# A two-layer graph network on one core: who copies edge weights and who adds them up in the sparse attention stage

## What is computed

```python
q = (z @ Wq.T + bq).reshape(n, H, D)          # n = 1250, H = 8, D = 64
k = (z @ Wk.T + bk).reshape(n, H, D)
v = (z @ Wv.T + bv).reshape(n, H, D)
s = einsum('ehd,ehd->eh', q[src], k[dst]) / sqrt(D) + att_bias   # one row per edge
m = segment_max(s, src)
p = exp(s - m[src])
denom = segment_sum(p, src)
alpha = p / where(denom[src] == 0, 1.0, denom[src])
agg = segment_sum(alpha[:, :, None] * v[dst], src)
att = agg.reshape(n, C) @ Wo.T + bo
x = x + att
```

## Time and profile before

| | us |
|---|---|
| median of 3 runs (2309.41 to 2314.92) | 2309.54 |
| the profiled execution, as timed | 2305.52 |
| its span in the profile | 2303.5 |
| busy: PE / DVE / ACT / POOL | 2067.1 / 1332.7 / 725.7 / 765.4 |
| attention stage, first multiply to last multiply | 681 to 1030 |

### The profile page before, as it was taken

The page is one execution under the profiler, slowest core; times in us unless marked ns, Lnnn a source line. Parts: engine busy times, 40 slices in busy tenths (PEclk is TensorE's granted clock), DMA queues, the critical chain, the costliest instruction groups (busy, mean ns, idle before and its releaser), DMA issues.

```text
span 2303.5 us, 31178 instructions
## 1 busy us (share of the span) xinstructions
PE 2067.1 (90%) x11980; PEld 1262.7 (55%) x11980; DVE 1332.7 (58%) x3173; ACT 725.7 (32%) x1551; POOL 765.4 (33%) x524
## 2 busy tenths in 40 slices
PE   4998987898988579998999999999999999999977
PEld 3555554443335345555775456677777754455554
DVE  5665687878969557772224544442222234279997
ACT  4221122320015345431222355554211102135552
POOL 1346878887864576450000000000000000014443
PEclk9998998999989889999999999999999999999999
DMA  9994232223249769655000010002200005000000
GB/s 321 386 374 105 13 66 3 3 3 65 3 69 219 149 160 242 176 148 176 1 1 10 1 74 1 1 1 92 92 1 1 1 6 145 0 1 10 10 14 14
DMA packets 105266, 181.95 MB, mean 79 GB/s; under 512 B 64600, under 2 KB 66290, under 8 KB 94910
## 3 DMA queue, kind: packets, MB, share of 16 engines
q1 hardware_dynamic: 60047, 178.50, 24.8%
q0 software_dynamic: 45072, 1.46, 5.7%
HBM read 109.21 MB, written 70.71 MB: 78 GB/s over the span
## 4 chain that ended last, share of the span: by engine, by line
PE 64%; DVE 10%; POOL 8%; DMA 8%; ACT 5%; issue 4%; SPq 2%; DVEq 0%; PEldq 0%; ACTq 0%; POOLq 0%; PEld 0%
PE banks L203 19%; POOL edge_table L622 7%; PE banks L2395 6%; PE banks L2437 6%; DMA edge_table<-arena 6%; PE banks L2821 3%; PE banks L1746 3%; PE banks L2223 2%; PE banks L2211 2%; PE banks L2198 2%; PE banks L197 2%; PE banks L1545 2%; PE banks L2247 2%; PE banks L1566 2%; DVE arena L1445 1%
## 5 line engine op out<-in xcount | busy, mean ns | idle before, releaser
L622 POOL DMA_INDIRECT edge_table<-arena x313 | 523.5, 1673 | 268.8 <-DMA edge_table<-arena 155.7
L203 PE MATMUL banks<-arena 128*125 128x512 f32 x1200 | 555.3, 609 | 16.9 <-DVE arena L3041 15.1
L203 PEld LDWEIGHTS banks<-arena 128*125 128x125 f32 x1200 | 221.7, 193 | 262.8 <-issue 244.9
L1445 DVE TENSOR_TENSOR arena<-banks,arena 125x1000 f32<-125x1000 f32 x100 | 193.9, 1955 | 82.8 <-POOL arena L1481 36.6
L2848 POOL CAST arena<-arena 125x128 f32<-125x128 uint32 x10 | 2.9, 292 | 699.5 <-DVE arena L2984 699.5
L1545 PE MATMUL banks<-arena 64*125 64x250 f32 x800 | 115.4, 408 | 67.3 <-DVE arena L1445 62.8
L2343 DVE SCALAR_TENSOR_TENSOR arena<-banks,arena 125x512 f32<-125x512 f32 x80 | 60.1, 751 | 189.4 <-PE banks L2437 189.4
L1481 POOL TENSOR_TENSOR arena<-arena 125x1000 f32<-125x1000 f32 x56 | 132.5, 2438 | 84.5 <-DVE arena L1445 84.5
L2395 PEld LDWEIGHTS banks<-arena 128*128 128x128 f32 x1280 | 144.0, 192 | 6.7 <-issue 6.6
L2090 DVE CUSTOM_DVE_ANT_0 arena<-banks,arena 125x512 f32<-125x512 f32 (+8 forms) x144 | 73.0, 553 | 128.7 <-PE banks L2198 125.9
L2395 PE MATMUL banks<-arena 128*128 128x125 f32 x1280 | 146.4, 276 | 0.1
(11 more groups left out here) (372 smaller groups left out, 3376.5 us busy)
## 6 DMA issues: line engine op xcount, KB each, us to landing
edge_table<-arena SPq DMA_DIRECT2D x23, 2304.0 KB, 25.9
arena<-edge_table SPq DMA_DIRECT2D x50, 984.4 KB
arena<-L_ffn_W SPq DMA_DIRECT2D x4, 2048.0 KB, 10.0
arena<-edge_table SPq DMA_DIRECT2D x50, 114.3 KB
adjacency<-arena SPq DMA_DIRECT2D x50, 109.4 KB
arena<-adjacency SPq DMA_DIRECT2D x10, 546.9 KB
edge_table<-arena POOLq DMA_INDIRECT x313
arena<-x SPq DMA_DIRECT2D x1, 2240.0 KB
```

The costliest lines, as they stand in the source:

```text
L203: last = nc.tensor.matmul(dst, xT[:, i, :], w[:, i, 0:n], start=(i == 0), stop=(i == k - 1))
L622: pool.indirect_dma_start(d["table"], bass.IndirectOffsetOnAxis(ap=cell[0:EP, c:c + 1].bitcast(U32), axis=0), vals[0:EP, c * ROW:(c + 1) * ...
L1445: nc.vector.tensor_tensor(weights_of(m).rearrange("p (s e n) -> p s e n", s=2, e=2), unit_scores(m).rearrange("p e (s n) -> p s e n", s=2) ...
```

## The change

Five things are changed at once.

1. A new ACT instruction for every unit (`copy_weights`) copies the four heads' weights of the block out of their nine-word records into a contiguous buffer (`copy_g[m % 2]`, 125x1000 fp32, head by head). It stands ahead of the unit's exponential in ACT's order and waits for the block to have landed and for the multiply of unit `m - 2`. DVE's multiply reads this buffer in place of the block, and waits for it (`a_w`).
2. `att_pool` is gone. DVE does `sum_weights` in all ten passes.
3. A block is loaded in three parts of 84, 83 and 83 sources, six DMAs in place of two.
4. SP loads block `i + 3` as soon as both copies and the gather of block `i` are done, and only then waits for the counts and stores them. The gather of a block now stands behind the exponential of its first unit.
5. X is stored by tiles, ten `spread`s in place of one.

```diff
             sp.wait_ge(g_ev, 3 * TILES)
-            spread(sp, d["x_kept"], X[0:TP, :, :].rearrange("p t c -> p (t c)"), s_x)
+            for t in range(TILES):
+                spread(sp, d["x_kept"][:, t * C:(t + 1) * C], X[0:TP, t, :], s_x)
...
+        BLOCK_PARTS = ((0, 84), (84, 167), (167, CHUNK))
...
-                spread(sp, edge_block(i)[0:TP, :, :], table[tok(b), sources(c), :], s_tab[i % RING])
+                for v, w in BLOCK_PARTS:
+                    spread(sp, edge_block(i)[0:TP, v:w, :], table[tok(b), c * CHUNK + v:c * CHUNK + w, :], s_tab[i % RING])
...
             for i in range(BLOCKS):
                 c, b = chunk_and_tile(i)
+                if i + RING < BLOCKS:
+                    sp.wait_ge(a_w, 2 * (i + 1))
+                    sp.wait_ge(a_ca, i + 1)
+                    load_block(i + RING)
                 sp.wait_ge(a_cc, i + 1)
                 spread(sp, adj_v[c][:, :, tok(b)], count_g[i % 2][0:TP, :, :], s_adj[i % 2])
-                if i + RING < BLOCKS:
-                    sp.wait_ge(a_p, 2 * (i + 1))
-                    load_block(i + RING)
...
-                if h == 0:
-                    block_loaded(dve, m // 2)
...
+                dve.wait_ge(a_w, m + 1)
                 dve.wait_ge(a_e, m + 1)
                 nc.vector.tensor_tensor(
                     weights_of(m).rearrange("p (s e n) -> p s e n", s=2, e=2),
                     unit_scores(m).rearrange("p e (s n) -> p s e n", s=2),
-                    edge_block(m // 2)[0:TP, :, 4 * h:4 * h + 4].rearrange("p n (s e) -> p s e n", s=2),
+                    copy_g[m % 2][0:TP, :].rearrange("p (s e n) -> p s e n", s=2, e=2),
                     ALU.mult).then_inc(a_p, 1)
-                if m >= 1 and place(m - 1)[1] and place(m - 1)[0] < DVE_PASSES:
-                    sum_weights(nc.vector, dve, m - 1)
+                if m >= 1 and place(m - 1)[1]:
+                    sum_weights(dve, m - 1)
...
+            def copy_weights(m):
+                h = place(m)[2]
+                if h == 0:
+                    block_loaded(act, m // 2)
+                if m >= 2:
+                    act.wait_ge(a_p, m - 1)
+                nc.scalar.activation(copy_g[m % 2][0:TP, :].rearrange("p (j n) -> p n j", j=4),
+                                     edge_block(m // 2)[0:TP, :, 4 * h:4 * h + 4], ACT.Copy).then_inc(a_w, 1)
...
-                if i >= 1 and h == 0:
-                    gather(i)
-                if m == 1:
-                    gather(0)
+                copy_weights(m)
                 act.wait_ge(a_s, m + 1)
                 nc.scalar.activation(unit_scores(m), unit_scores(m), ACT.Exp).then_inc(a_e, 1)
-                if h == 0 and i >= 1:
-                    count_out(i - 1)
+                if h == 0:
+                    gather(i)
+                    if i >= 1:
+                        count_out(i - 1)
```

More of the change, by code:

```diff
@@ L124, in gps_two_layers @@
         s_const = sem("constants_ready")
-        s_x = sem("x_loaded")
+        s_x = sem("x_loaded_and_stored")
+        X_STORED = 32 + 32 * TILES
         z_rows, z_turned, z_cols = sem("z_ready"), sem("z_transposed"), sem("zT_ready")
@@ L1300, in gps_two_layers @@
         assert 33792 + 2 * CHUNK * ROW <= 36864 + CLEAR * ROW
-        DVE_PASSES = 3
         values_kept = arena[:, 0:CHUNKS * PAIRS * CHUNK].rearrange("p (c j n) -> p c j n", c=CHUNKS, j=PAIRS)
@@ L1305, in gps_two_layers @@
         count_g = [space.take(CHUNK).rearrange("p (u n) -> p u n", u=2) for _ in range(2)]
-        space = Space(BUF, BUF + 4616)
+        copy_g = [space.take(4 * CHUNK)]
+        space = Space(BUF, BUF + 4616 + 240)
         plain_g = [space.take(CHUNK) for _ in range(2)]
@@ L1309, in gps_two_layers @@
         rden = space.take(CHUNK)
+        copy_g.append(space.take(4 * CHUNK))
         s_tab = [sem(f"table_block_loaded_{i}") for i in range(RING)]
@@ L1315, in gps_two_layers @@
         a_e = sem("att_exponentials_ready")
+        a_w = sem("att_edge_weights_copied")
         a_p = sem("att_weights_ready")
@@ L1360, in sources @@
             return slice(c * CHUNK, (c + 1) * CHUNK)
+        BLOCK_PARTS = ((0, 84), (84, 167), (167, CHUNK))
         def block_loaded(eng, i):
-            eng.wait_ge(s_tab[i % RING], 32 * (i // RING + 1))
+            eng.wait_ge(s_tab[i % RING], 32 * len(BLOCK_PARTS) * (i // RING + 1))
         def att_sp(sp):
@@ L1396, in att_sp @@
                 if v == 1:
-                    sp.wait_ge(s_x, 96)
+                    sp.wait_ge(s_x, X_STORED + 32)
                 spread(sp, flat_x[:, a:b], d["x_kept"][:, a:b], s_x)
@@ L1462, in att_dve @@
                                 divide(g - CHUNKS - 1, half)
+            sum_weights(dve, UNITS - 1)
             for u in range(2):
@@ L1471, in att_dve, with sum_weights @@
             leave_stage(dve, "DVE")
-        def sum_weights(ops, eng, m):
+        def sum_weights(dve, m):
             g, n, h = place(m)
-            eng.wait_ge(a_p, m + 1)
+            dve.wait_ge(a_p, m + 1)
             if n == 1:
-                eng.wait_ge(a_pv, m - 1)
+                dve.wait_ge(a_pv, m - 1)
             else:
-                eng.wait_ge(a_sum, m - 2 * (g + 1) - 1)
+                dve.wait_ge(a_sum, m - 2 * (g + 1) - 1)
             total_p = psum_g[g % 2][0:TP, 2 * h:2 * h + 2, :].rearrange("p s n -> p (s n)")
-            ops.tensor_tensor(total_p, total_p, weights_of(m), ALU.add).then_inc(a_sum, 1)
-        def att_pool(pool):
-            pool.wait_ge(a_sum, ADDS * DVE_PASSES)
-            for m in range(PER * DVE_PASSES, UNITS):
-                if place(m)[1]:
-                    sum_weights(nc.gpsimd, pool, m)
+            nc.vector.tensor_tensor(total_p, total_p, weights_of(m), ALU.add).then_inc(a_sum, 1)
         def att_act(act):
@@ L1493, in copied @@
                 if g == 0:
-                    act.wait_ge(s_x, 64)
+                    act.wait_ge(s_x, X_STORED)
                 out = qT_g[:, :, sources(c)] if late else values_kept[:, c, :, :]
@@ L1498, in copied @@
                                      .rearrange("p b (j n) -> p b j n", j=2), ACT.Copy).then_inc(a_raw, 1)
+            def copy_weights(m):
[6 more added lines that the diff above has]
+                                     edge_block(m // 2)[0:TP, :, 4 * h:4 * h + 4], ACT.Copy).then_inc(a_w, 1)
             def gather(i):
                 c, b = chunk_and_tile(i)
-                block_loaded(act, i)
                 if i >= 2:
@@ L1679, in ff_dve @@
                 if t == 0:
-                    dve.wait_ge(s_x, 96)
+                    dve.wait_ge(s_x, X_STORED + 32)
                 if t == X_EARLY:
-                    dve.wait_ge(s_x, 128)
+                    dve.wait_ge(s_x, X_STORED + 64)
                 link(dve, nc.vector.tensor_tensor(X[0:TP, t, :], X[0:TP, t, :], XN[0:TP, t, :], ALU.add))
@@ L3275, in _ @@
             edges_pool(pool)
-            att_pool(pool)
             causal_pool(pool)
```

## The result

| | before | after |
|---|---|---|
| median, us (5 executions each, side by side) | 2309.41 | 2294.72 (2293.42 to 2296.95) |
| profiled execution, us | 2305.52 | 2294.18 |
| its span, us | 2303.5 | 2292.4 |
| busy PE / DVE / ACT / POOL, us | 2067.1 / 1332.7 / 725.7 / 765.4 | 2073.3 / 1316.2 / 898.0 / 629.5 |

The ratio of the times is 0.9935, with an interval of 0.9912 to 0.9957. The kernel became faster by 0.65%, some 15 us by the medians and 11.3 us between the two profiled executions. The forecast was 2269 us, a gain of 40. So the sign and the range held, and the size was off by 26 us. The 4 us by which I raised the sum to a median were therefore mostly chance, and the gain against those medians is nearer to 10 us.

The account below looks back on a forecast made before the run. Taken as bounds: a 36 us stall on POOL's order, DVE in early passes, PE in later ones. From 2305.5 us, -37 up to pass 6 and -3 late give 2265, plus 4.0 for the median 2269 us; range 2256 to 2313.

Parts of the forecast that it names:

- The 4 us by which I raised the sum to a median: Whole kernel: 2265 us summed from the profiled execution became 2269, since the earlier median stood 4.0 us above that execution.
- The copy: New ACT instruction per unit: 1.1 us each, between bounds of 1.03 and 2.0, making ACT's block about 5.5 us.
- The start: Unit 0: copy and exponential now stand behind block 0's landing, 1.1 + 1.0 and half a us for issues, +2.6 us.
- The sum: First multiply to pass 6: 2.6 + 16 x 5.9 + 14 x 5.5 = 174 us against 211.5, -37; late passes -3.
- The doubled copy: Rival, chance 0.22: scattered writes make ACT's copy 1.95 us; 2321 us, turning to loss at about 1.85 us a copy.
- The late passes: Passes 6 to 9: the shorter DVE multiply counts once a pass behind the inverse, -0.8 us each, -3 in all.
- The stall: Attention stage: 36.0 us of waiting for POOL's sum, queued behind its scatters, is freed with the sums on DVE.
- The term of 7 us: Store of X near 544: packets of 2048 bytes save POOL some 7 us of its 12, four scatters, leaving 39 at 681.
- The part on the blocks: Scatters beside block loads in 3024-byte parts: 5.1 us for two in flight, 2.5 us a scatter, against 3.8 before.
- my 778: Table scatters: the remaining 39 at 2.5 us each end at about 778, before block 25 is wanted (about 805).
- DMA as the limit: Rival, chance 0.15: added small packets at 0.1 us each make blocks 6.3 us, 7.5 beside scatters; 2293 us.
- The term of 5.9 us a block: First 16 attention blocks: loads slowed by scatters, 4.99/0.84 = 5.9 us a block, making DMA the limit above ACT's 5.5.

Follow-up runs that it names:

- large packets: The changed kernel with blocks loaded whole (9000 bytes) and X stored whole (20480 bytes): median 2296.2 us, ratio 0.9959.
- half early, all late: The changed kernel with copies for the second unit of each block only in passes 0 to 5, all in passes 6 to 9: 2263.2 us, ratio 0.9814.
- the same with whole blocks: The kernel "half early, all late" with blocks loaded whole, X still stored by tiles: 2286.6 us, ratio 0.9926.
- the kernel with pairs: The changed kernel with two heads' words side by side in the copy buffer, DVE reading with 8-byte stride: 2257.8 us, ratio 0.9794.

## Why the prediction was right in sign and wrong in size

*The copy: the step that failed.* The term was 1.1 us for a copy. The trace has 1.90 us for the first one, which stands alone (the timeline under "The start"), and 2.117 on average. Timeline of ACT over a block of pass 1, and a copy of pass 7:

```profile
734.75 2.09 ACT L1508 ACTIVATE arena<-arena 125x1000 f32<-125x1000 f32 x1
736.51 1.22 ACT L1531 ACTIVATE banks<-banks 125x1000 f32<-125x1000 f32 x1
737.53 2.08 ACT L1508 ACTIVATE arena<-arena 125x1000 f32<-125x1000 f32 x1
739.27 1.23 ACT L1531 ACTIVATE banks<-banks 125x1000 f32<-125x1000 f32 x1
740.29 0.78 ACT L1515 ACTIVATE arena<-arena 125x250 f32<-125x250 f32 x1
740.83 0.33 ACT L1515 ACTIVATION_READ_ACCUMULATOR arena<-arena 125x1 f32 x1
740.92 0.51 ACT L1522 ACTIVATE arena<-banks 125x250 f32<-125x250 f32 x1
741.18 2.10 ACT L1508 ACTIVATE arena<-arena 125x1000 f32<-125x1000 f32 x1
...
930.10 1.97 ACT L1508 ACTIVATE arena<-arena 125x1000 f32<-125x1000 f32 x1
```

I had both bounds, 1.03 and 2.0 us, and chose the lower end by DVE's fill of one word in nine. It was the wrong neighbour: another engine, and no input to read. The right one was ACT's own row with scattered writes, line 554, which I had priced at 1.8 ns an element; the copy has (1900 - 205)/1000, 1.7. A rule for the next time is to take the neighbour on the same engine and with the same side strided, even where its type differs. The Trainium skill ("SBUF — State Buffer", section "Door 1: The DMA port swizzle") asks for at least two hits on each line of 16 bytes. The runs agree, for ACT's writes as for DVE's reads: with one word in a line the copy takes 1.90 us alone and the multiply 1.967, and two words side by side are enough (1.185 and 1.193 us).

*The sum.* From 734.75 to 741.18 a block takes 6.43 us, and with a fifth of the values' copy (1.0 us) 6.63, that is 33.2 a pass. The sum had 5.9 for 16 blocks and 5.5 for 14, on average 5.71. Timeline of DVE at the first multiply of pass 6, before and after:

```profile
886.80 1.98 DVE L1445 TENSOR_TENSOR arena<-banks,arena 125x1000 f32<-125x1000 f32 x1 [0.67 <-ACT banks L1524]
...
879.55 1.20 DVE L1452 TENSOR_TENSOR arena<-banks,arena 125x1000 f32<-125x1000 f32 x1 [0.44 <-ACT banks L1531]
```

From the first multiply at 682.05 the thirty blocks took 197.5 us, where the sum had 171.4: 26.1 us more. A second step failed as well, in the base of the sum. I read the start of pass 6 as 892.5, the end of a stretch in the earlier trace rows, but its first multiply starts at 886.80. So before, the thirty blocks took 205.8 us and not 211.5, and the forecast held 5.7 us of gain that wasn't there. The start took 1.1 us and not 2.6, and from pass 6 to the end 3.9 us were gained and not 3. So of the sum's 40.5 us (37.5 and 3) there remain 40.5 - 26.1 - 5.7 + 1.5 + 0.9 = 11.1, and the two spans differ by 11.1.

*The doubled copy, as a rival.* Its mechanism is what happened, near its price of 1.95 us, but its time, 2321 us, was wrong, and so was its turning point. It added durations. In the changed kernel's early passes ACT's instructions overlap: by the starts above a copy takes 1.75, an exponential 1.02, the gather with its accumulator 0.63 and the counts 0.26, where I had 1.95, 0.99, 0.84 and 0.38 less 0.1 in all. The block is 6.6 us and not 7.15, some 16 us less over thirty. And the late passes didn't become longer, to 39 us, but shorter: ACT is busy for 33.56 us of 35.60 and fits in, while the multiply, 0.75 us shorter, is worth more than the copy costs.

*The late passes.* The term was -0.8 a pass, and -2.0 is measured (37.6 to 35.6). I had let the shorter multiply count once, where PE waits behind the inverse, and set the two at the divisions against DVE's new sums. In the trace of after the divisions themselves are shorter as well:

```profile
936.96 0.68 DVE L1426 TENSOR_TENSOR arena<-arena 128x500 f32<-128x500 f32 x1
```

Before, it took 1.04 us on average. The run with POOL's sums in the late passes shows the place of it (1.93 us beside a sum of POOL, 0.67 without). The Trainium skill ("SBUF — State Buffer", section "Who interferes with whom") says that a DVE instruction with two inputs in SBUF contends with a GpSimd instruction that reads SBUF. The trace agrees, and also in that the multiply, with one input in PSUM, stays at 1.196 us. But that run has passes of 35.6 us all the same, so the multiply carries the gain. In total the term was nearly right, by luck: four passes 2.0 us shorter would be 8 us, but from the first multiply of pass 6 to that of pass 7 it takes 34.7 us, where before it took 31.1. I haven't followed that first late pass.

*The stall* was POOL's order, as forecast, and is gone. Timeline of POOL at the store of X, and in the attention stage:

```profile
542.70 6.85 POOL L623 DMA_INDIRECT edge_table<-arena  x1 [0.30 <-issue]
549.85 1.66 POOL L623 DMA_INDIRECT edge_table<-arena  x1 [0.30 <-issue]
553.86 1.54 POOL L623 DMA_INDIRECT edge_table<-arena  x1 [2.35 <-DMA edge_table<-arena]
557.56 1.54 POOL L623 DMA_INDIRECT edge_table<-arena  x1 [2.17 <-DMA edge_table<-arena]
...
776.58 1.54 POOL L623 DMA_INDIRECT edge_table<-arena  x1 [1.93 <-DMA edge_table<-arena]
...
782.21 1.65 POOL L623 DMA_INDIRECT edge_table<-arena  x1 [2.24 <-DMA edge_table<-arena]
...
790.12 1.54 POOL L623 DMA_INDIRECT edge_table<-arena  x1 [1.18 <-DMA edge_table<-arena]
```

The gap of 11.96 us at X is gone, but three gaps of 7.15, 4.01 and 3.70 us stand in its place. Starts usually lie 1.85 us apart, so the three cost 9.3 us, and before, from 542.60 to 560.57, four cost 10.6. The term of 7 us was wrong; about 1 us is saved. That 38 scatters were left at 681, near the 39 forecast, has another reason: 203 had started by 535, where before it were 200, and from there to 681 it was 72 and 70. A number that comes true doesn't show its reason. The part on the blocks holds in direction: a pair takes 5.6 us (forecast 5.1, before 7.6). But part of that is the longer pass. From 681 to 788 the changed kernel gets 37 scatters through, and 31 with large packets; with passes of 27.3 us it is 33 ("half early, all late") and 25 (the same with whole blocks). So small packets at short passes give 107/33 = 3.2 us a scatter, where I had 2.5. The last one starts at 790, later than my 778 and before my limit of 800. That block 25 would be wanted at 805 was wrong in the changed kernel, whose blocks come later, and right for a fast one: with passes of 25.6 us the last scatter goes out at 811.75 and the wait is 13.58 us. So the scatters aren't independent of the pace of loads. At blocks of 4.91 us 33 of them get through in 107 us, at 6.43 us 37.

*DMA as the limit.* Queues from 700 to 770, columns as in the earlier trace rows:

```profile
q1 hardware_dynamic: 7969, 13.29, 68.3%
q0 software_dynamic: 3600, 0.12, 11.4%
```

That is 0.683 x 70 = 47.8 us for 70/6.63 = 10.6 blocks, 4.5 us a block against 4.74 before: the added packets cost nothing, and this rival had no ground. The term of 5.9 us a block beside scatters was wrong too. In the kernel with pairs blocks come every 4.91 us beside scatters, at a share of 1.03. It is the scatters that give way, not the loads.

*The start.* Timelines of ACT and DVE at the first unit:

```profile
677.72 1.90 ACT L1508 ACTIVATE arena<-arena 125x1000 f32<-125x1000 f32 x1 [8.63 <-DMA arena<-edge_table]
679.63 1.28 ACT L1531 ACT_TABLE_LOAD   x1
680.93 0.99 ACT L1531 ACTIVATE banks<-banks 125x1000 f32<-125x1000 f32 x1
...
682.05 1.20 DVE L1452 TENSOR_TENSOR arena<-banks,arena 125x1000 f32<-125x1000 f32 x1 [17.65 <-ACT banks L1531]
```

From the landing of block 0 to the multiply it is 4.3 us. I had 2.6, with a copy of 1.1, and without the load of ACT's tables (1.28 us), which stood in the shadow of the DMA before and now stands behind the copy. The multiply starts only 1.1 us later than before, since block 0 had landed 3.2 us earlier (677.7 against 680.9). The whole stage had begun earlier: PE's first scores start at 669.23, before at 672.31. Nothing in the diff accounts for that. In the traces of the experiments they start anywhere from 666.26 to 671.27, so it may be no more than how executions differ.

*A forecast tested with its own price.* The kernel with pairs has the copy that I had assumed (1.185 us), and gains 37.6 us by pass 5, where I had forecast 37, and 46.5 in all. The agreement is in part luck: the passes are shorter than I had put them (25.6 us, not 27.5 to 29.5), the table's wait takes back 13.6, and the 37 held the 5.7 us of the base. Yet it shows that the price of the copy was the step on which the forecast stood.

## What to carry to other kernels

When a copy is to free one engine of a strided operand, look at both of its sides: here single words 1000 bytes apart on the writing side cost ACT about what the other engine saved, and writing them in pairs, which the reader can still take at full speed, was worth 37 us. Price an engine that may fill up by start-to-start times and not by durations, since a few tenths for each instruction decided here between a gain and a loss. Take both ends of the stretch that a sum is set against from the same event: here one end was read off a window, and 5.7 us of the forecast gain were never there. And a removed stall is gone only as far as the next resource lets it: an edit that is worth nothing in one version (small packets, 0 us) can be worth 24 us in the next, so it should be measured again once the passes are shorter.

## What the runs showed of the hardware

- ACT writing single fp32 words 1000 bytes apart takes 1.90 us for 1000 when alone, in runs of two or four words 1.18 us; beside such single writes, reading four words of nine or contiguously makes no difference (2.117 and 2.108 us on average). DVE's multiply takes 1.97 us with a stride of 16 bytes and 1.19 with one of 8 or none. Whether the size of the line or something else of the port sets the limit wasn't tried beyond these strides.
- Loads in packets of 3024 bytes were as fast as in packets of 9000 (4.5 and 4.74 us a block), and the small scattered transfers beside them sped up: in the kernel with passes of 27.3 us 33 in place of 25 got through in 107 us.
- In the changed kernel the recorded durations of ACT stretch: the exponential has 0.99 us at its shortest, 1.24 on average and 1.59 at most, though in the block shown its starts lie 1.02 before the next. The mean of 2.117 us for the copy is such a number, too; the starts give 1.75. A full engine isn't enough for it: in the kernel with pairs ACT is as full (28.92 of 29.0 us), and the exponential has 1.00 us on average and 1.03 at most. The cause stays open.
- A DVE addition of 500 fp32 with both inputs in SBUF took 0.67 us without POOL's sums beside it and up to 1.93 with them; the multiply of the same size with an input in PSUM took 0.68 in all three kernels looked at (before, changed, and with POOL's sums late).
